# Graph attention block on one Trainium2 core: V made one step behind its scores, turns of eight steps, x loaded beside stores of probabilities

## The reference

```
q = x @ Wq + bq;  k = x @ Wk + bk;  v = x @ Wv + bv
probs = softmax(q k^T / 8 + (0 where adj, else -9e15))      per head, over k
ctx   = probs @ v                                           heads put side by side
out   = layernorm(x + ctx @ Wf + bf)                        over the 384 features, no scale or shift
```

## Time and profile before

| | us |
|---|---|
| median of three runs | 1043.46 |
| the profiled execution, its own time | 1043.48 |
| span of its trace | 1041.7 |
| TensorE busy | 1018.5 (98%) |
| VectorE / GpSimd / ScalarE busy | 733.8 / 631.1 / 593.2 |
| one step in the middle | 15.68 |
| mean granted TensorE clock | 0.993 |

### The profile page before, as it was taken

The page is one execution under the profiler, slowest core; times in us unless marked ns, Lnnn a source line. Parts: engine busy times, 40 slices in busy tenths (PEclk is TensorE's granted clock), DMA queues, the critical chain, the costliest instruction groups (busy, mean ns, idle before and its releaser), DMA issues.

```text
span 1041.7 us, 26751 instructions
## 1 busy us (share of the span) xinstructions
PE 1018.5 (98%) x7161; PEld 907.3 (87%) x7161; DVE 733.8 (70%) x2823; ACT 593.2 (57%) x2119; POOL 631.1 (61%) x652
## 2 busy tenths in 40 slices
PE   8999999999999999999999999999999999999975
PEld 7889889889888888889889889889888888888864
DVE  3576777777777777677677677677677677677564
ACT  3565655655655655655656656656656656656550
POOL 1356666666656656656656656656666665665675
PEclk9999999999999999999999999999999999999988
DMA  7266566666666666666666666666666666665443
GB/s 199 64 157 174 172 179 175 182 177 177 179 183 173 180 181 173 180 184 173 179 183 171 180 184 176 179 181 180 178 179 177 178 177 179 183 184 184 144 145 114
DMA packets 338970, 179.63 MB, mean 172 GB/s; under 512 B 222592, under 2 KB 322560, under 8 KB 338944
## 3 DMA queue, kind: packets, MB, share of 16 engines
q1 hardware_dynamic: 338544, 178.74, 62.0%
q10 hardware_dynamic: 400, 0.59, 0.2%
HBM read 103.75 MB, written 75.50 MB: 172 GB/s over the span
## 4 chain that ended last, share of the span: by engine, by line
PE 96%; DVE 2%; POOL 1%; DMA 1%; issue 1%; ACT 0%; SPq 0%; DVEq 0%; POOLq 0%
PE qk_ps L338 14%; PE cov_ps L338 13%; PE cov_ps L340 13%; PE cov_ps L339 13%; PE qk_ps L340 13%; PE qk_ps L339 13%; PE scores_ps L354 9%; PE cov_ps L368 8%; DMA x_in<-in_x 1%; DVE s_mask L500 0%; DVE stats L538 0%; DVE y_sb L532 0%; DVE wv_lo L468 0%; DVE p_turned L512 0%; POOL x_bias L702 0%
## 5 line engine op out<-in xcount | busy, mean ns | idle before, releaser
L628 ACT ACTIVATE probs<-s_mask,neg_max 128x128 f32<-128x128 f32 x768 | 297.5, 391 | 6.9 <-DVE neg_max L506 6.9
L500 DVE CUSTOM_DVE_ANT_0 s_mask<-scores_ps,mask_bias 128x128 f32<-128x128 f32 x768 | 172.5, 287 | 95.7 <-PE scores_ps L354 91.2
L719 POOL TENSOR_TENSOR probs<-probs,inv_sum 128x768 f32<-128x768 f32 x128 | 188.7, 1474 | 80.0 <-DVE inv_sum L519 80.0
L714 POOL TENSOR_SCALAR y_sb<-y_sb,mean_var,rstd 128x384 f32<-128x384 f32 x127 | 209.8, 1652 | 23.4 <-POOL rstd L708 23.4
L512 DVE STREAM_TRANSPOSE p_turned<-probs 128x768 f32<-128x768 f32 x128 | 125.2, 978 | 116.0 <-POOL probs L719 116.0
L708 POOL TENSOR_TENSOR rstd<-var_eps,minus_half 128x1 f32<-128x1 f32 x128 | 71.9, 562 | 179.3 <-DVE var_eps L544 179.3
L646 ACT ACTIVATE qT<-qk_ps,bq_col 128x512 f32<-128x512 f32 x96 | 65.5, 683 | 154.3 <-PE qk_ps L340 154.3
L628 ACT ACTIVATION_READ_ACCUMULATOR probs<-s_mask,neg_max 128x1 f32 x768 | 145.1, 189 | 0.0
L338 PE MATMUL cov_ps<-wf_hi,cT_hi 128*128 128x384 f32 x384 | 131.0, 341 | 11.6 <-DVE cT_lo L474 11.6
L621 ACT CAST cT_hi<-cov_ps 128x384 fp32r<-128x384 f32 x128 | 61.5, 480 | 137.7 <-PE cov_ps L368 134.9
L489 DVE TENSOR_TENSOR xT_lo<-xT,xT_hi 128x384 fp32r<-128x384 f32 x120 | 112.9, 979 | 33.1 <-ACT xT_hi L615 32.9
(11 more groups left out here) (57 smaller groups left out, 1974.6 us busy)
## 6 DMA issues: line engine op xcount, KB each, us to landing
p_out<-p_turned SPq DMA_DIRECT2D x128, 384.0 KB, 2.9
pT<-p_out SPq DMA_DIRECT2D x512, 96.0 KB, 2.2
x_in<-in_x SPq DMA_DIRECT2D x128, 192.0 KB, 2.6
out<-y_sb SPq DMA_DIRECT2D x128, 192.0 KB, 2.1
x_blocks<-in_x SPq DMA_DIRECT2D x360, 64.0 KB, 2.2
adj_u<-in_adj SPq DMA_DIRECT2D x32, 64.0 KB, 2.1
y_sb<-in_L_gnn_Wq ACTq DMA_DIRECT2D x1, 576.0 KB, 4.7
s_mask<-in_L_gnn_Wk SPq DMA_DIRECT2D x1, 576.0 KB, 6.6
```

What stands on the lines that cost most here:

```text
L500: last = nc.vector.tensor_tensor_reduce(out=s_mask[:, e, h, :], in0=scores_ps[:, score_cols(e, h)], in1=mask_bias[:, e, :], scale=SCALE, s ...
L628: last = nc.scalar.activation(probs[:, e, h, :], s_mask[:, e, h, :], ACT.Exp, bias=neg_max[:, e, h:h + 1], scale=1.0, accum_out=row_sum[:, ...
L714: nc.gpsimd.tensor_scalar(y_sb[:, y, :], y_sb[:, y, :], mean_var[:, e, 0:1], rstd[:, e, 0:1], ALU.subtract, ALU.mult).then_inc(y_ready, 1)
L719: nc.gpsimd.tensor_tensor(probs[:, e, :, :], probs[:, e, :, :], inv_sum[:, e, :].unsqueeze(2).broadcast_to([P, HEADS, SEQ]), ALU.mult).the ...
```

## The change

V of a pair is made at step p for pair p - 1 instead of pair p + 2, as the last product of the step as before. So the split x has to be kept longer: `xT_hi` and `xT_lo` get four slots of a group instead of two, and a turn is eight steps, so that slot numbers are constants within it (TURN_GROUPS = 4). V's first wait in the banks is for the bias row, which is now made in `cov_ps[0]`, so the scores of pair 0 no longer wait for it. wv is split at step -1, behind wf. On SyncE the `x_in` loads and the adjacency go to the front of the step (the adjacency without a wait of its own), and the six `x_blocks` loads go between the store of graph 2p and its reads.

```diff
-TURN = 4
+TURN = 8
+V_LAG = 1
+XT_RING = 4
+TURN_GROUPS = TURN * 2 // GROUP
-        xT_hi = sb("xT_hi", [P, 2, KC, GTOK], F32R)
-        xT_lo = sb("xT_lo", [P, 2, KC, GTOK], F32R)
+        xT_hi = sb("xT_hi", [P, XT_RING, KC, GTOK], F32R)
+        xT_lo = sb("xT_lo", [P, XT_RING, KC, GTOK], F32R)
...
@@ SyncE, step @@
+                if real(p + X_LEAD, PAIRS) and not by_matmul(2 * (p + X_LEAD)):
+                    for e in range(2):
+                        load_x(2 * (p + X_LEAD) + e, (2 * (c + X_LEAD) + e) % X_RING)
+                if c % 2 == 0 and real(p + 2, PAIRS):
+                    g, slot = TURN_GROUPS * i + c // 2 + 1, (c // 2 + 1) % 2
+
+                    sp.dma_start(adj_u8[:, slot, :, :],
...
                 if real(p - 1, PAIRS):
                     load_blocks(i, c - 1, 1, 2 * (p - 1) + 1)
...
-                if c % 2 == 0 and real(p + 2, PAIRS):
-                    g, slot = 2 * i + c // 2 + 1, (c // 2 + 1) % 2
-                    past(sp, masked_ready, 2 * (p - 1) + 1)
-                    sp.dma_start(adj_u8[:, slot, :, :],
...
+                if real(p, PAIRS):
+                    store_blocks(c, 0, 2 * p)
                 if real(p + BLOCKS_AHEAD, PAIRS) and not by_matmul(2 * (p + BLOCKS_AHEAD - c % 2)):
                     load_x_blocks(i, c, c % 2)
-                if real(p + X_LEAD, PAIRS) and not by_matmul(2 * (p + X_LEAD)):
-                    for e in range(2):
-                        load_x(2 * (p + X_LEAD) + e, (2 * (c + X_LEAD) + e) % X_RING)
                 if real(p, PAIRS):
-                    store_blocks(c, 0, 2 * p)
                     load_blocks(i, c, 0, 2 * p)
                     store_blocks(c, 1, 2 * p + 1)
@@ TensorE @@
                     if isinstance(n, int) and n == 0:
                         past(pe, xT_split, BY_MATMUL - 1)
-                        pe.wait_ge(bias_row_ready, 1)
...
-                if isinstance(p, int) and p - 1 + AHEAD >= PAIRS:
-                    past(pe, y_added, n - 2)
-                else:
-                    past(pe, v_copied, 2 * (p - 1 + AHEAD) + e)
+                past(pe, v_copied, n)
...
             def v_product(c, p, e):
-                n, at = 2 * (p + AHEAD) + e, 2 * (c + AHEAD) + e
-                par, tok = at // GROUP % 2, tokens(at)
+                n, at = 2 * (p - V_LAG) + e, 2 * (c - V_LAG) + e
+                par, tok = at // GROUP % XT_RING, tokens(at)
...
                 if real(p - LAG, PAIRS):
                     past(pe, y_added, 2 * (p - LAG) + e)
-                else:
-                    past(pe, v_copied, n - 2)
+                elif e == 0:
+                    pe.wait_ge(bias_row_ready, 1)
...
-                past(pe, xT_split, GROUP)
                 for k in range(KC):
-                    last = nc.tensor.matmul(xT_bank(0)[:, 0:HID], bv_wide[:, k, :], w_raw["f"][:, k, :],
+                    last = nc.tensor.matmul(cov_ps[0][:, 0:HID], bv_wide[:, k, :], w_raw["f"][:, k, :],
                                             start=k == 0, stop=k == KC - 1)
...
-                if real(p + AHEAD, PAIRS):
+                if real(p - V_LAG, PAIRS):
                     for e in range(2):
                         v_product(c, p, e)
@@ VectorE, step @@
-                if early and p == -2:
-                    split_weight("v")
                 if early and p == -1:
                     dve.wait_ge(bias_mm, 1)
...
                     split_weight("f")
+                    split_weight("v")
@@ ScalarE, step @@
-                if real(p + AHEAD, PAIRS):
-                    for e in range(2):
-                        copy_v(c, e, 2 * (p + AHEAD) + e)
+                if real(p - V_LAG, PAIRS):
+                    for e in range(2):
+                        copy_v(c, e, 2 * (p - V_LAG) + e)
```

More of the change, by code:

```diff
@@ L254, in load_x_blocks @@
             def load_x_blocks(i, c, half):
-                g = 2 * i + (c + BLOCKS_AHEAD) // 2
+                g = TURN_GROUPS * i + (c + BLOCKS_AHEAD) // 2
                 slot = (c + BLOCKS_AHEAD) // 2 % 2
@@ L299, in step @@
                     load_weight(sp, "f", wf)
+                if real(p + X_LEAD, PAIRS) and not by_matmul(2 * (p + X_LEAD)):
[4 more added lines that the diff above has]
+                    sp.dma_start(adj_u8[:, slot, :, :],
+                                 adj[bass.ds(g * GROUP, GROUP), :, :].rearrange("b q k -> q b k")
+                                 ).then_inc(adj_loaded[slot], DMA)
                 if real(p - 1, PAIRS):
@@ L345, in scores @@
                 if e == 0:
-                    past(pe, qk_copied, 2 * i + c // 2, per=NJ)
+                    past(pe, qk_copied, TURN_GROUPS * i + c // 2, per=NJ)
                     if isinstance(n, int) and n == 0:
                         past(pe, xT_split, BY_MATMUL - 1)
-                        pe.wait_ge(bias_row_ready, 1)
                 past(pe, max_found, n - 2)
@@ L359, in ctx_product @@
                 n, at = 2 * (p - LAG) + e, 2 * (c - LAG) + e
-                past(pe, pT_landed[at % PT_RING], 2 * i + at // PT_RING, per=BLOCKS * DMA)
-                if isinstance(p, int) and p - 1 + AHEAD >= PAIRS:
-                    past(pe, y_added, n - 2)
-                else:
-                    past(pe, v_copied, 2 * (p - 1 + AHEAD) + e)
+                past(pe, pT_landed[at % PT_RING], 2 * TURN // PT_RING * i + at // PT_RING, per=BLOCKS * DMA)
+                past(pe, v_copied, n)
                 dst = cov_ps[e]
@@ L374, in qk_product @@
                 mat, m = QK_JOBS[j]
-                g, par = 2 * i + (c + AHEAD) // 2, (c + AHEAD) // 2 % 2
+                g, par = TURN_GROUPS * i + (c + AHEAD) // 2, (c + AHEAD) // 2 % XT_RING
                 if isinstance(g, int) and g == 0:
@@ L479, in turn_x @@
                 par, b = at // GROUP % 2, at % GROUP
-                past(dve, x_blocks_loaded[par], i + (at - BY_MATMUL) // (2 * GROUP), per=KC * BLOCKS * DMA)
+                past(dve, x_blocks_loaded[par], TURN_GROUPS // 2 * i + (at - BY_MATMUL) // (2 * GROUP), per=KC * BLOCKS * DMA)
                 past(dve, xT_split, n - 2)
@@ L530, in add_residual @@
                 else:
-                    dve.wait_ge(y_stored[y], (2 * i + at // Y_RING) * DMA)
+                    dve.wait_ge(y_stored[y], (2 * TURN // Y_RING * i + at // Y_RING) * DMA)
                 nc.vector.tensor_tensor(y_sb[:, y, :], cov_ps[e][:, 0:HID], x_bias[:, at % X_RING, :], ALU.add
@@ L575, in step @@
                         split_x(c, e, 2 * (p + X_AHEAD) + e)
-                if early and p == -2:
-                    split_weight("v")
                 if early and p == -1:
                     dve.wait_ge(bias_mm, 1)
-                    nc.vector.tensor_tensor(bias_row[:, :], xT_bank(0)[:, 0:HID], bf_row[:, :], ALU.add
+                    nc.vector.tensor_tensor(bias_row[:, :], cov_ps[0][:, 0:HID], bf_row[:, :], ALU.add
                                             ).then_inc(bias_row_ready, 1)
                     split_weight("f")
+                    split_weight("v")
                 if real(p - LAG, PAIRS):
@@ L612, in round_x @@
                     past(act, x_turned, n - BY_MATMUL)
-                past(act, qk_done, 2 * i + at // GROUP - 2, per=NJ)
-                past(act, v_done, n - 2 * GROUP)
+                past(act, qk_done, TURN_GROUPS * i + at // GROUP - XT_RING, per=NJ)
+                past(act, v_done, n - XT_RING * GROUP)
                 nc.scalar.copy(xT_hi[:, par, :, tok], xT_source(n, e)).then_inc(xT_hi_ready, 1)
@@ L633, in copy_v @@
             def copy_v(c, e, n):
-                slot = (2 * (c + AHEAD) + e) % V_RING
+                slot = (2 * (c - V_LAG) + e) % V_RING
                 past(act, v_done, n)
@@ L641, in copy_qk @@
                 mat, m = QK_JOBS[j]
-                g, par = 2 * i + (c + AHEAD) // 2, (c + AHEAD) // 2 % 2
+                g, par = TURN_GROUPS * i + (c + AHEAD) // 2, (c + AHEAD) // 2 % 2
                 past(act, qk_done, g * NJ + j)
@@ L691, in make_mask_bias @@
                 par = at // GROUP % 2
-                past(pool, adj_loaded[par], i + at // (2 * GROUP), per=DMA)
+                past(pool, adj_loaded[par], TURN_GROUPS // 2 * i + at // (2 * GROUP), per=DMA)
                 past(pool, max_found, n - 2)
@@ L699, in add_bias @@
                 slot = (2 * c + e) % X_RING
-                past(pool, x_loaded[slot], i, per=DMA)
+                past(pool, x_loaded[slot], 2 * TURN // X_RING * i + (2 * c + e) // X_RING, per=DMA)
                 past(pool, y_added, n - X_RING)
```

2 lines of the change are left out of this document (removed).

## The result

The changed kernel takes 1050.96 us (median of six runs, 1050.11 to 1051.32), the kernel before, run on the same chip, 1045.13. The ratio is 1.0057 with an interval of 1.0043 to 1.0071: slower, by about 6 us or 0.6%. The time is that of its third rival, the larger loop body, priced there at 1052 with a chance of 0.15.

The account below looks back on a forecast made before the run. TensorE was taken to bound head and middle, the softmax chain and VectorE's order the loose tail. From 1043.48: -7.2 (head) + 1.6 (clock) + 1.8 (tail) = -3.8, so 1039.7 us, range 1036.5 to 1046.

Parts of the forecast that it names:

- third rival: Loop's jumps back: eight steps don't stay in TensorE's or VectorE's instruction memory; 1052 us at 2.5 a jump, chance 0.15.
- Turns of eight steps: Loop's five jumps back: the longer body costs 0, bounds 0 and 23 us for exposed code fetches.
- Head: Before the first scores: V of pairs 0 and 1 leaves steps -2 and -1, 7.2 us less, scores at 26.5.
- V(2) in step 0: Head, step 0: removing this 3.25 us product gains 0, since q2 of step 1 waits for ScalarE's k1 copy.
- The clock behind that stall: Step 1: TensorE's 3.2 us stall brings a half-clock stretch, costing 1.6 us (bounds 0 and 3.4).
- Tail: Steps 62 to 64: V of pairs 61, 62 and 63 comes in, 1.8 us more (bounds -0.3 and +3.4).
- SyncE: Its queue in the middle: the moved loads stand in its waits for stores, cost nothing, with room.
- Middle: Steps between head and tail: same matmuls in the same order, 15.68 us a step stays, change 0.

Follow-up runs that it names:

- e1: The changed kernel with every engine's steps written out, no hardware loop: 1039.16 us against 1042.68 for the kernel before.
- e7: The kernel before with turns of eight steps on all engines and SyncE in the new order: 1078.43 us.
- e11: The changed kernel written out, with V of a pair made in the pair's own step: 1036.55 us.
- e4: The changed kernel with TensorE's steps alone written out, the other engines in loops of eight steps: 1054.22 us.
- e5: The changed kernel with every step written out and SyncE's queue in the order of the kernel before: 1053.70 us.
- e8: The changed kernel with TensorE alone in its loop of eight steps, the other four engines written out: 1047.11 us.
- e14: The changed kernel with 100 waits that are long met put ahead of TensorE's step -4: 1057.81 us.
- e12: The kernel before in its turns of four steps, with SyncE's new order alone: 1042.90 us.
- e6: The kernel before with every step written out and SyncE in the new order: 1042.75 us.

## Why the prediction was wrong

**The step that failed** is "Turns of eight steps ... I take 0, since a fetch can run while the engines still work through what they hold". It cost 12.2 us: 1050.96 in the loop, 1039.16 without it (e1). Half of the reason was true: of TensorE's 4.3 us behind its branch 2.7 were hidden. The other half failed on VectorE and ScalarE: they have just finished their step there and have no issued work left that would cover 3.8 us, and the slack in front of the mask was only 1.3 to 1.4 us of idle time in the trace before. The bounds given, 0 to 23 us, held, and so did the rival's price of 2.5 a jump; it had too small a chance, and the range ended at 1046, 6 us below its time. That the price came out so close (2.35 to 2.53 measured) is in part luck: the same body of eight steps cost 6.6 to 8.2 us a jump in e7, where TensorE's code lay otherwise. The Trainium skill's rule ("Runtime: NRT & Kernel Launch", Instruction fetch mechanics: a jump out of the window stalls for the fetch) is what the trace shows for eight steps, 3.6 to 4.3 us on four engines; for four steps the trace shows 0.3 and no fetch. The rule calls the window two pages, which the section gives as blocks of 16 KiB; a TensorE body of about 58 KB (an estimate, below) was kept all the same, and there the measurement decides.

**What could have been read before.** Up to the end of its first turn the kernel before brought code at a rate, and the body's size could be had from it: q8's six packets of 16 KB in 125 us are about one a step or somewhat less. (The prediction read these alone; q14 brought ten of 8 KB beside them.) e1 gives the rate over a longer stretch: 44 packets for 49 steps, by which I estimate 14.6 KB a step for TensorE, 58 KB for four steps, which stay, and 117 KB for eight, which don't. A doubled body was the largest unknown of the change, and zero was its most hopeful value.

**Head: right.** First scores at 25.85 instead of 26.5, 0.7 sooner than summed, and 0.6 of that is no part of the change: the first Q/K matmul started at 9.21 us instead of 9.79, and it starts anywhere from 9.2 to 10.1 in the traces of the other kernels without added waits. From that matmul to the first scores it took 16.64 us instead of 23.94: 7.3 less, for 7.2. V(2) in step 0 was worth nothing, as said: q2 of step 1 waited 2.88 us for the copy (3.2 predicted) and began 16.9 us behind the first scores (17.1). e11 is the proof by use: V put into that gap costs 0.3 us there (22.55 to step 2, against 22.28 in e1).

**The clock behind that stall: right in the profiled run,** 1.3 us instead of 1.6. In e4, e5, e8 and e14 a stretch of 3.4 us at granted 0.50 stands there too. In e1 the same stall of 2.8 us was followed by none, and step 2 came 22.3 us behind step 0: such a stall decides nothing for certain.

**Tail: right in the two profiled runs, in part by luck,** 1.7 us for 1.8. Against e12 and e6, whose TensorE does in the tail what it did before and which lack the second half-clock stretch of the earlier trace rows, it is 2.7 us. V(61) waited 1.36 us for the residual, V(62) 0.64, and the stall in front of out(61) shrank from 5.97 to 2.21 us at full clock.

**SyncE: right for the loops, and short of the point.** Worth 0 there (e12). But I read SyncE's waits as "4.9 us of a step" to be filled and didn't add its issues to them: it waited for next to nothing else (0.4 us between 180 and 900 us), so it had no slack at all. That shows once code is written out, where the new order is worth 14.5 to 18 us.

**Middle: right.** 15.68 us a step away from the jumps.

## What to carry to other kernels

A longer loop body is a change of its own: look at the instruction queues of the profile for whether the present body is fetched at all in the loop, work out bytes per step from the first turn, and count a jump out of what is held at several us on every engine whose body is fetched anew, on those that have just drained their work above all. An engine that waits only for its own DMAs has no slack, even if nobody waits for it yet. And where the head is full and the tail is loose, move work from the one to the other by the smallest step that the buffers allow, before buying room with a longer turn.

## What the runs showed of the hardware that was not expected

- A jump back takes 0.3 us on VectorE with a body of four steps and 3.8 with one of eight, while GpSimd's stays at 0.2 to 0.3 with both; TensorE's body of some 58 KB stayed, one of some 117 KB did not (estimates). Straight code was fetched beside the work at no cost where SyncE had slack: e6 and the kernel before differ by a factor of 1.0002.
- Where TensorE's code lies matters: 48 waits that do nothing, ahead of the first step, took 22.6 us off a kernel (1078.43 to 1055.80).
- Taking TensorE out of the loop made the kernel slower (1054.22 for 1050.96), since the other engines' jumps then stood alone: 2.4 to 3.6 us each, for 2.35 to 2.53.
